# Columns 1 and 2 of rows 14 and 15 by seven products ahead of time, in a two-layer graph kernel

## The reference

```python
def L0(x, adj, u):                       # first layer
    keep = (u >= 0.1).astype(x.dtype)
    return adj @ (x * keep / 0.9)
def L1(x, adj, weight, bias):            # second layer
    return adj @ (x @ weight) + bias
x = layernorm(x + L0(x, adj, u))         # this is h
x = layernorm(x + L1(x, adj, weight, bias))
```

## Time and profile before

| | |
|---|---|
| median of 3 runs | 892.34 us (892.27 to 892.49) |
| profiled execution, its own time | 892.4 us |
| its span, first to last instruction | 890.6 us |
| TensorE busy | 859.6 us, 97% |
| VectorE busy | 553.2 us, 62% |
| moved by DMA | 357.63 MB, mean 402 GB/s |
| loads of 1024 KB tiles in the main part | 306 |

### The profile page before, as it was taken

How to read it: one execution, slowest core, us unless ns; L and a number is a source line. 1 busy time by engine, 2 the same in 40 slices (tenths; PEclk the granted TensorE clock), 3 DMA queues, 4 the chain that set the end, 5 groups by cost and what they waited for, 6 DMA issues and landing times.

```text
span 890.6 us, 15637 instructions
## 1 busy us (share of the span) xinstructions
PE 859.6 (97%) x6742; PEld 498.5 (56%) x6742; DVE 553.2 (62%) x1132; ACT 25.5 (3%) x63; POOL 25.3 (3%) x24
## 2 busy tenths in 40 slices
PE   2899899999999999999999999999999999999996
PEld 2565564445576676675756464564645645556432
DVE  6366123145135676787677777776877868787755
ACT  2100000000000000000000000000000000000011
POOL 3000000000000000000000000000000000000133
PEclk9999999999999999999999999999999999999998
DMA  9999999999999999999999999999989999999972
GB/s 373 413 415 420 422 421 419 421 421 420 420 410 424 419 421 421 418 420 368 422 421 420 407 421 379 423 390 394 422 363 421 421 418 421 420 420 421 421 299 71
DMA packets 53108, 357.63 MB, mean 402 GB/s; under 512 B 6192, under 2 KB 8240, under 8 KB 10288
## 3 DMA queue, kind: packets, MB, share of 16 engines
q1 hardware_dynamic: 53040, 356.64, 96.9%
HBM read 354.52 MB, written 2.10 MB: 400 GB/s over the span
## 4 chain that ended last, share of the span: by engine, by line
PE 91%; DMA 5%; SPq 1%; issue 1%; DVE 1%; POOLq 0%; POOL 0%; ACT 0%; DVEq 0%
PE psum L1031 22%; PE psum L984 22%; PE psum L999 8%; PE psum L967 8%; PE psum L993 8%; PE psum L1017 8%; DMA tiles<-adj_chunks 5%; PE psum L953 4%; PE psum L974 4%; PE psum L1037 4%; PE psum L930 1%; SPq L499 1%; PE psum L995 1%; PE psum L969 1%; PE psum L1001 1%
## 5 line engine op out<-in xcount | busy, mean ns | idle before, releaser
L984 PE MATMUL psum<-tiles,stat 128*64 128x256 f32 x1952 | 218.0, 379 | 0.0
L1031 PE MATMUL psum<-tiles,stat 128*64 128x512 f32 x944 | 210.0, 593 | 0.0
L656 DVE TENSOR_TENSOR layer<-psum,layer 128x512 f32<-128x512 f32 (+1 forms) x147 | 101.4, 690 | 170.3 <-PE psum L1017 65.2
L984 PEld LDWEIGHTS psum<-tiles,stat 128*64 128x64 f32 x1952 | 158.2, 137 | 59.4 <-issue 8.6
L1031 PEld LDWEIGHTS psum<-tiles,stat 128*64 128x64 f32 x944 | 70.8, 137 | 117.1 <-issue 113.5
L692 DVE TENSOR_TENSOR tiles<-tiles 128x512 f32<-128x512 f32 x86 | 59.4, 691 | 52.1 <-PE psum L976 50.6
L1001 PE MATMUL psum<-tiles,stat 128*64 128x256 f32 x344 | 88.5, 380 | 0.0
L969 PE MATMUL psum<-tiles,stat 128*64 128x256 f32 x344 | 88.3, 379 | 0.0
L967 PE MATMUL psum<-tiles,stat 128*64 128x256 f32 x344 | 88.3, 379 | 0.0
L1017 PE MATMUL psum<-tiles,stat 128*64 128x512 f32 x320 | 70.4, 593 | 3.1 <-issue 3.1
L967 PEld LDWEIGHTS psum<-tiles,stat 128*64 128x64 f32 x344 | 47.1, 137 | 34.9 <-issue 16.5
(11 more groups left out here) (99 smaller groups left out, 866.5 us busy)
## 6 DMA issues: line engine op xcount, KB each, us to landing
tiles<-adj_t SPq DMA_DIRECT2D x306, 1024.0 KB, 13.0
tiles<-adj SPq DMA_DIRECT2D x12, 1024.0 KB, 19.3
tiles<-adj_chunks SPq DMA_DIRECT2D x12, 1024.0 KB, 21.4
tiles<-xu SPq DMA_DIRECT2D x4, 1024.0 KB, 8.1
tiles<-adj_parts SPq DMA_DIRECT2D x16, 256.0 KB, 17.9
out<-layer SPq DMA_DIRECT2D x8, 256.0 KB, 2.2
w<-weight SPq DMA_DIRECT2D x4, 16.0 KB, 9.0
bias_b<-bias SPq DMA_DIRECT2D x1, 32.0 KB, 9.4
```

Source lines behind the costliest of these rows:

```text
L656: return dve.tensor_tensor(out=to, in0=addend, in1=to, op=ALU.add)
L984: last = pe.matmul(sum_f[i % 2][to, left], stat[:, j * C + c, 0:D], tile[:, c, columns], start=begun.get("f") != i and c == 0, stop=ends a ...
L1031: last = pe.matmul(bank[to, :], stat[:, j * C + c, D:2 * D], tile[:, c], start=c == 0, stop=c == C - 1)
```

## The change

`early` jobs remain for column 1 on rows 2 to 13 (and for (14, 0)). Columns 1 and 2 of rows 14 and 15 become products, worked in row 3 as two groups, `GROUPS_AHEAD = {3: ((15, (1, 2)), (14, (1, 2)))}`, each followed by a combination of its own. Column 2 of rows 12 and 13 becomes products in these rows. `sum_stat` is made for column 1 too, for which there is one more home of 2 KB a partition. A group is placed when row 3's own combination stands in the list, at least `APART` = 5 choices of the loop have been made since the last combination and the lead is below 32, or when neither light, heavy nor due jobs are left. The wait of a group's first `raw` now counts the combinations in the list, and a combination ends a group.

```diff
-MORE_FROM = (12,)
-HOMES = (NB - 2 - EARLY) // 2
+EARLY_COLUMNS = 1
+GROUPS_AHEAD = {3: ((15, (1, 2)), (14, (1, 2)))}
+ROWS_AHEAD = {r: columns for groups in GROUPS_AHEAD.values() for r, columns in groups}
+APART = 5
+HOMES = (NB - 2 - EARLY) // 2 + 1
...
 def begins_at(i):
-    return EARLY + sum(i >= row for row in MORE_FROM) if i >= EARLY else 0
+    if i in ROWS_AHEAD:
+        return ROWS_AHEAD[i][-1] + 1
+    return EARLY if i >= EARLY else 0
...
-        if 1 <= i - 1 < EARLY:
-            early = sorted(early + [("early", r, i - 1) for r in range(EARLY, NB, 2)], key=lambda job: job[1:])
-        if EARLY <= i - 1 < EARLY + len(MORE_FROM):
-            early = sorted(early + [("early", r, i - 1) for r in range(MORE_FROM[i - 1 - EARLY], NB, 2)], key=lambda job: job[1:])
+        if EARLY_COLUMNS <= i - 1 < EARLY:
+            early = [("early", r, i - 1) for r in range(EARLY, NB, 2) if r not in ROWS_AHEAD]
         if i >= 2 and begins_at(i) < i:
             heavy.append(double(i, i - 1))
+        ahead = [[*(("fused", r, j) for j in columns), ("combine", r, 0)] for r, columns in GROUPS_AHEAD.get(i, ())]
+        since = APART
...
             due = [job for job in early if job[1] == i]
-            if not (heavy or light or due):
+            if not (heavy or light or due or ahead):
                 break
+            if summed and ahead and (since >= APART and lead < LEAD or not (light or heavy or due)):
+                for job in ahead.pop(0):
+                    if job[0] == "combine":
+                        jobs.append(job)
+                    else:
+                        put(job)
+                        if light:
+                            put(light.pop(0))
+                since = 0
+                continue
+            since += 1
...
             if not summed and not any(job[0] == "fused" for job in heavy):
-                jobs.append(("combine", i))
+                jobs.append(("combine", i, 1))
+                since = 0
                 summed = True
...
-            home = layer1_pair(j) if j % 2 else stat_homes[:, (j - EARLY) // 2]
+            home = layer1_pair(j) if j % 2 and j > EARLY else stat_homes[:, j // 2]
...
-                if EARLY <= i < NB - 2:
+                if EARLY_COLUMNS <= i < NB - 2:
                     sum_stat(i)
...
                     if kind == "raw":
-                        new = begun.get("products") != i
-                        begun["products"] = i
+                        new = not begun.get("products")
+                        begun["products"] = True
                         if new:
-                            pe.wait_ge(combined, 2 * combined_rows(i - 1))
+                            pe.wait_ge(combined, 2 * n_combined)
...
+                if kind == "combine":
+                    n_combined += 1
+                    begun["products"] = False
```

More of the change, by code:

```diff
@@ L303, in resnorm_graph_layers @@
     loads, place = place_tiles(jobs)
-    def combined_rows(i):
-        return sum(has_fused(r) for r in range(i + 1))
     done_after, n_tile_jobs = {}, 0
@@ L880, in _ @@
             stat_sums_seen = 0
+            n_combined = 0
             begun = {}
@@ L894, in stat_sums_of @@
                 nonlocal stat_sums_seen
-                if j - EARLY + 1 > stat_sums_seen:
-                    pe.wait_ge(stat_sums_ready, j - EARLY + 1)
-                    stat_sums_seen = j - EARLY + 1
+                if j - EARLY_COLUMNS + 1 > stat_sums_seen:
+                    pe.wait_ge(stat_sums_ready, j - EARLY_COLUMNS + 1)
+                    stat_sums_seen = j - EARLY_COLUMNS + 1
             def h_of(turned_rows):
@@ L1053, in _ @@
                         pe.wait_ge(turned_read, turns(NB - 1))
-                        pe.wait_ge(combined, 2 * combined_rows(NB - 1))
+                        pe.wait_ge(combined, 2 * n_combined)
                     pe.wait_ge(added, complete[i])
```

## The result

The changed kernel takes 896.48 us (median of 4 runs, 895.72 to 897.16); the kernel before takes 892.41 (892.27 to 892.49). The ratio is 1.0046, 95% interval 1.0033 to 1.0058: slower by 4.1 us. Forecast was 895.5 with 893.8 to 897.5. The profiled execution took 896.0 us with a span of 894.2, 3.6 more than before.

What follows compares the result with a forecast made beforehand. From 209 us TensorE bounds the kernel, with DMA nearly full. Span 890.6 - 2.5 (six tiles) + 4.3 (pause) + 1.4 (clock) = 893.8, so the median 892.34 + 3.2 = 895.5 us; range 893.8 to 897.5.

Steps and rivals of the forecast that it cites:

- Order by hand: Row 3: TensorE runs first(3, 13), combine(15), first(3, 14), raw(14, 1), so one "first" of 1.73 us covers the combination.
- Six tiles: Six tiles turned from early into products, in rows 3, 12 and 13, save 0.415 us each on TensorE, 2.5 us together.
- The pause: Near 233 us in row 3, raw(14, 1) waits for row 15's combination: 6.03 us less one "first", 4.3 us; bounds 4.1 to 5.0.
- The loads: Row 3 loses 3.5 us of load lead; without the pause TensorE waits about 1.9 us for DMA in rows 5 and 6.
- tile (6, 15): Tightest tile found behind row 3: lands at 331.5 us, its matmuls begin at 333.3, leaving 1.6 to 1.8 us of lead.
- The clock: The pause in row 3 likely drops TensorE's granted clock to the half rate, costing 1.4 us; bounds 0 and 3.4.
- The upper bound of 3.4: Most that the clock's fall was taken to cost, in us, if the half rate lasts over two such stretches and more.
- the 2.3 us pause near 90 us: TensorE pause in the kernel before, at 90.2 us, where the granted clock stays 1.00; the forecast pause is nearly twice it.
- VectorE: About 25 us more VectorE work on 553, nearly all in row 3, costed at nothing on the path except in the pause.
- The signs named ahead: One 4 to 5 us pause near 233 us, half clock or none, row 4 earlier, row 14 later, no DMA wait rows 5, 6.

Runs made afterwards that it cites:

- experiment 1: The changed kernel with row 15's combination ahead of time cut to its last two additions (row 15's sums not computed): 892.38 us, ratio 1.000.
- experiment 5: The changed kernel, but early(12, 2) stays and is worked between row 15's combination and raw(14, 1): 891.37 us, ratio 0.9988.
- experiment 6: The changed kernel with no "first" jobs inside groups, so three instead of one lie between row 15's combination and raw(14, 1): 892.12 us, ratio 0.9996.
- 8: The changed kernel with six more unused copies on VectorE ahead of row 15's combination, to lengthen the pause: 898.79 us.
- 3: The kernel before with only column 2 of rows 12 and 13 turned into products; rows 14 and 15 stay early: 892.54 us, ratio 1.0001.
- experiment 2: The changed kernel with 8 unused matmuls of 512 columns put ahead of raw(14, 1)'s wait, filling the pause: 894.14 us.
- experiment 7: The changed kernel itself, run again unchanged to see its spread: 895.91 us, ratio 1.004.
- experiment 4: The changed kernel without groups ahead: columns 1 and 2 of rows 14 and 15 become products in their own rows: 894.09 us, ratio 1.0019.

## Why the prediction was right

- **Order by hand: right.** combine(15), one "first", raw(14, 1), as derived; the second condition lets the group through because the light jobs are used up. That was the step on which the sign hung.
- **Six tiles: 2.5 us.** Seen in 1: 8.6 us less in row 3 and 3.02 us more for each of the two products in rows 12 and 13, so 2.6.
- **The pause: 4.3 us forecast, 4.12 measured as idle** and 4.3 from where the next job was due. Experiments 1, 5 and 6 take it away, or most of it, by its cause; 8 lengthens it by as much as VectorE works longer.
- **The loads: 1.9 us hidden behind the pause.** It could not be seen in the changed kernel, and 1 showed it: 2.2 us. The place was off: in 1 the jobs that wait are in row 5, not at tile (6, 15), which was the tightest found from a single load; in 3 it is (6, 15). That pause and loads replace each other and do not add is shown by 6.
- **The clock: right in kind, small in size.** Forecast 1.4, measured 1.7 (profile) and 1.8 (experiment 2). This term is the mis-sized one, by 0.3 us. The 1.4 came from the first 32 matmul records of the kernel, of which only those up to 16.9 us were slow (0.42 us a record, then 0.27); in row 3 all 3.4 us at half rate were worked. The upper bound of 3.4 was not worked out either: two such stretches make 2.8. The median of the first set, 896.48, is 1.0 above the forecast; 0.7 of that stands in the two runs near 897 and is not explained, and without them (experiment 7, 895.91) the forecast is 0.4 off.
- **One argument was false,** though its conclusion held. I took the 2.3 us pause near 90 us for one that leaves the clock alone. In experiments 1, 4 and 8 the clock fell near the end of that same pause (half rate from 93.7, 93.1 and 92.4 us). What stands is that the longer pause brought the fall each time it was profiled. Windows of experiment 1:

```profile
90.00:93.60 3.60, 1.17 (x8) 0.50 (x8) 0.00 (x0) 0.00 (x0) 0.00 (x0) 1.00 1.01 419
93.70:97.00 3.30, 3.30 (x10) 1.17 (x8) 0.00 (x0) 0.00 (x0) 0.00 (x0) 0.50 1.02 422
97.20:99.00 1.80, 1.80 (x10) 0.69 (x8) 0.00 (x0) 0.00 (x0) 0.00 (x0) 1.00 0.99 414
```

It cost nothing there: raw(3, 2) begins between 207.9 and 208.1 us with it, and between 208.0 and 208.3 without it. Without it TensorE waits 0.5 us at 134.3 (for DMA) and 0.8 to 0.9 us at 190.1; in the three executions with it both waits are gone, so this part of the kernel had time to give back.

- **VectorE: 575.9 us, 23 more**, forecast about 25; no wait on the path but the one.
- **The signs named ahead:** one pause near 233 us ended by the combination, the half rate behind it, and no wait for DMA in rows 5 and 6 came as named. Row 4 begins 2.4 us earlier (forecast 3 with the fall) and row 14 begins 3.6 us later (forecast 2 to 3); both are off by the clock's term and by the 0.1 us that row 3 started later. The sum gives 3.2 for row 14, so that "2 to 3" was read too low from it.

## What to carry to other kernels

Work in groups that share one accumulator needs, between two groups, at least as much other work as emptying it takes (here 6.0 us with both hand-overs). A planner that counts jobs as distance must also check that the jobs exist, or hold some back: here one early job of 6.9 us, kept and worked between the two groups, turns +3.5 us into -1.0, with four tiles turned into products and not six. Where two resources are nearly full, price a cheaper job against both: 8.5 us less matrix work with 5.0 us less loads uses up 3.5 us of lead, and a lead of 1.6 us pays for no more. A pause can hide such a shortage, and taking the pause away then gains less than its length: with the clock full in both, experiment 1 has a span 2.1 us under that of experiment 2 (890.2 against 892.3), for a pause of 4.3.

## What the runs showed of the hardware

- A TensorE pause of 4.1 us brought the half rate in both profiled executions of the changed kernel, 0.6 us after work had begun again, for 3.4 us. A pause of 6.1 us brought it in the one profiled execution, from 3.0 us before work began again, for 6.8 us. A pause of 0.7 us did not (experiment 6). A pause of 2.2 to 2.5 us near 90 us did so in 3 of 10 profiled executions and not in the other 7, and its length does not tell which: 2.17 us was followed by the half rate (experiment 4), 2.47 us was not (experiment 5).
- Matmuls whose result is thrown away, put into such a pause, make the kernel faster by 1.8 us (895.91 to 894.14).
- Time at the half rate costs only where it is worked and where nothing waits anyway: 3.4 us of it cost 1.7 us in row 3 and nothing near 90 us.
- The run-to-run spread of 0.9 to 1.1 us in experiments 3 and 5 (before 0.5 to 0.6) is in good part outside the span: the spans spread over 0.5 and 0.7 us, those of the kernel before over 0.6. That the lead at zero widens the spread is not shown; experiment 1, where the loads do bind, spreads over 0.6.
